# A projection of twelve matmuls dealt out in four pieces between the taps of a sampled stencil

## What is computed

```python
x = x + _L0_conv_ref(_gn(x), ...)        # deformable 3x3 convolution, 8 groups
t = t + _L1_attn_ref(_ln_t(t), L1_attn_W)  # attention over the 1024 pixels of an image
t = t + _L1_ffn_ref(_ln_t(t), ...)       # top 2 of 8 experts, per image, layer norm
```

```python
xp = x @ in_w + in_b
x1 = silu(batch_norm(depthwise_conv3x3(x)))
offset = x1 @ off_w + off_b
mask = softmax((x1 @ mask_w + mask_b).reshape(N, H, W, G, P), -1)   # G = 8, P = 9
samples = _bilinear_sample(img, sg)      # xp at 9 shifted points of each pixel and group
out = (samples * m).sum(-1)
return out @ out_w + out_b
```

## Time and profile before

| | us |
|---|---|
| median of 3 runs | 719.99 |
| lowest, highest | 719.28, 720.27 |
| the profiled execution | 716.8 |
| its span | 714.9 |
| PE, DVE, POOL, ACT busy in it | 588.3, 580.3, 304.6, 227.3 |

### The profile page before, as it was taken

One profiled execution on the slowest core, in us unless ns is written; L12 is line 12 of the kernel. 1 busy time (PEld: TensorE's weight loads), 2 busy tenths in 40 slices (PEclk: granted clock), 3 DMA queues, 4 the chain that ended last, 5 costly groups with the idle time before them and its releaser, 6 DMA issues.

```text
span 714.9 us, 11099 instructions
## 1 busy us (share of the span) xinstructions
PE 588.3 (82%) x3456; PEld 440.8 (62%) x3456; DVE 580.3 (81%) x1052; ACT 227.3 (32%) x334; POOL 304.6 (43%) x326
## 2 busy tenths in 40 slices
PE   5973877869859959969968689889999999939995
PEld 4542656558547547557547577667777777725674
DVE  4589999998999997998999999826777766652766
ACT  6150602413315205205207000234545444413431
POOL 6524794897448792058068240201222121115111
PEclk9996999998999988989999679999999999967998
DMA  6067403003003006000000000000000000004111
GB/s 184 30 260 255 141 1 104 3 1 105 1 1 105 2 2 257 1 1 2 1 1 3 0 1 1 0 1 1 1 1 1 1 1 0 1 9 110 30 45 44
DMA packets 25594, 30.54 MB, mean 43 GB/s; under 512 B 5188, under 2 KB 17684, under 8 KB 25556
## 3 DMA queue, kind: packets, MB, share of 16 engines
q1 hardware_dynamic: 24654, 29.77, 12.6%
q0 software_dynamic: 896, 0.23, 0.4%
q10 hardware_dynamic: 6, 0.00, 0.0%
HBM read 24.94 MB, written 5.05 MB: 42 GB/s over the span
## 4 chain that ended last, share of the span: by engine, by line
PE 54%; DVE 21%; issue 11%; DVEq 2%; ACT 1%; POOL 0%; POOLq 0%; ACTq 0%
PE banks L797 13%; DVE prod L1389 9%; PE banks L910 8%; PE pair L890 8%; PE pair L966 4%; PE pair L750 4%; PE banks L900 4%; PE banks L1000 3%; DVE stencil L1365 3%; DVE outer L1359 3%; PE banks L819 2%; PE pair L743 2%; PE banks L816 1%; PE banks L882 1%; PE banks L861 1%
## 5 line engine op out<-in xcount | busy, mean ns | idle before, releaser
L797 PE MATMUL banks<-ident,prod 128*128 128x128 f32 x1568 | 224.6, 294 | 82.6 <-DVE prod L1389 81.6
L797 PEld LDWEIGHTS banks<-ident,prod 128*128 128x128 f32 x1568 | 191.5, 152 | 137.8 <-DVE prod L1389 114.4
L1389 DVE TENSOR_TENSOR prod<-shifted,stencil 128x1024 f32 (+1 forms) x224 | 238.4, 1086 | 14.9 <-PE banks L797 14.6
L1157 POOL CAST far_list_i<-far_list 1x8 int32<-1x8 f32 x8 | 40.2, 5026 | 105.9 <-DVE far_list L1375 86.5
L1185 POOL TENSOR_TENSOR rstd_now<-mv_now,neg_half 128x2 f32<-128x2 f32 x32 | 23.0, 718 | 132.6 <-DVE mv_now L1441 132.6
L750 PE MATMUL pair<-xg,dw_diag 128*128 128x512 f32 x144 | 72.7, 606 | 1.2 <-ACT dw_diag L514 1.2
L910 PEld LDWEIGHTS banks<-shifted 128*128 128x128 f32 x512 | 60.2, 192 | 8.1 <-issue 6.1
L910 PE MATMUL banks<-shifted 128*128 128x128 f32 x512 | 63.2, 277 | 2.3 <-ACT shifted L651 1.4
L1359 DVE TENSOR_TENSOR outer<-hats 128x800 f32<-128x800 f32 x64 | 63.2, 987 | 0.8
L1365 DVE TENSOR_TENSOR stencil<-stencil,outer 128x800 f32 (+1 forms) x64 | 62.9, 982 | 0.3
L890 PE MATMUL pair<-shifted 128*128 128x512 f32 x128 | 60.8, 597 | 0.7 <-ACT shifted L634 0.6
(11 more groups left out here) (230 smaller groups left out, 837.0 us busy)
## 6 DMA issues: line engine op xcount, KB each, us to landing
shifted<-padded SPq DMA_DIRECT2D x42, 256.0 KB
shifted<-padded SPq DMA_DIRECT2D x14, 640.0 KB
res<-in_x_dram SPq DMA_DIRECT2D x4, 512.0 KB, 5.8
padded<-stage SPq DMA_DIRECT2D x4, 512.0 KB, 2.6
stage<-in_L_ffn_W_dram SPq DMA_DIRECT2D x16, 128.0 KB, 2.1
out_dram<-res SPq DMA_DIRECT2D x8, 256.0 KB, 2.3
padded<-stencil SPq DMA_DIRECT2D x2, 228.0 KB, 2.5
got<-padded,cell_now POOLq DMA_INDIRECT x28
```

The costliest lines, as they stand in the source:

```text
L797: mm = pe.matmul(acc_of(c, r), prod[:, d % PROD, r * G:(r + 1) * G, :].rearrange("p g c -> p (g c)"), ident[:, :], is_transpose=True, star ...
L1157: gp.tensor_copy(far_list_i[:, :], far_list[:, :]).then_inc(point, 1)
L1389: ins = ve.tensor_tensor(prod[:, dx:dx + n, :, :], shifted[:, dx:dx + n, bass.ds(((c % HALF) * ROWS + dy) * G, ROWS * G), :], stencil_of[: ...
```

## The change

The far sums of the chunk before move from ahead of tap 36 to ahead of tap 35. The projection of that chunk moves from ahead of tap 44, where its twelve matmuls stood in one row, to four places: the three matmuls of image 0 ahead of tap 39, of image 1 ahead of 41, of image 2 ahead of 43 and of image 3 ahead of 45. Every piece waits for the copy of the samples and for the residual of the chunk before it; only the last raises `conv_out`, for which ACT's `residual` waits. The two projections behind the last turn stay as they are, with their semaphore now named at the call.

```diff
-AT_FAR, AT_CONV, AT_SAMPLES, AT_PROJECT = 18, 22, 36, 44
+AT_FAR, AT_CONV, AT_SAMPLES, AT_PROJECT = 18, 22, 35, 39
...
-            def project(k, n0=0, n1=B):
+            def project(k, n0, n1, done=None):
                 last = isinstance(k, int) and k == CHUNKS - 1
                 pe.wait_ge(samp_t_done, k + 1)
                 pe.wait_ge(res1_done, CHUNKS - 1 if last else k + 1)
-                if n0 > 0:
+                if n0 > 0 and done is not None and n1 - n0 > 1:
                     pe.wait_ge(res1_first, 2 if last else 1)
...
-                mm.then_inc(conv_out if n1 == B else conv_first, 1)
+                if done is not None:
+                    mm.then_inc(done, 1)
...
-                    if i == AT_PROJECT and not first:
-                        project(k - 1)
+                    n, between = divmod(i - AT_PROJECT, 2)
+                    if 0 <= n < B and between == 0 and not first:
+                        project(k - 1, n, n + 1, conv_out if n == B - 1 else None)
                     add_up(k, i, i + 1)
...
-            project(CHUNKS - 2, 0, 1)
-            project(CHUNKS - 1, 0, 1)
+            project(CHUNKS - 2, 0, 1, conv_first)
+            project(CHUNKS - 1, 0, 1, conv_first)
...
-            project(CHUNKS - 2, 1, B)
-            project(CHUNKS - 1, 1, B)
+            project(CHUNKS - 2, 1, B, conv_out)
+            project(CHUNKS - 1, 1, B, conv_out)
```

## The result

The changed kernel takes 709.12 us (median of 4 runs, 706.93 to 709.60), the kernel before 719.63 us (median of 4 runs in this comparison, 716.62 to 720.27). The ratio is 0.986, with a 95% interval of 0.983 to 0.989: 10.5 us less. A second comparison, 5 runs against 17, gave 707.19 against 718.81 us, ratio 0.984 (0.981 to 0.987). The profiled execution took 709.08 us, its span 707.3 us.

A forecast was written before the change was run, and what follows sets the result against it. The stage was taken as bound by DVE, lengthened by PE where no `prod` slot was free. The profiled 716.8 us less 7.0 gave 709.8, plus 3.2 carried over to the median 713.0; range 708.5 to 718.0.

The forecast's parts named there:

- the lag rule: At a turn end, DVE's stall is the offset matmuls' delay behind `finish_silu`'s end without the first stall, plus 0.2 us.
- The floor of 0.6 us a turn end: DVE's stall with offset matmuls but no projection, as in turn 0; ACT's hat chain would hold DVE at `weigh_hats` anyway.
- The signs it named: DVE's slot waits 3.5 to 7.5 us, one stall of 0.5 to 1.5 per turn end, `finish_silu` spacing 50.1 to 51.
- Far sums zero: Four transposes moved from tap 36 to tap 35 hide in PE's wait as before: zero gain.
- switches zero: Going between transposes and projection matmuls on PE costs zero, upper bound 0.1 us each, 0.3 us a turn.
- copy of the samples in time: No piece waits for the samples' copy: 1.8 us of room ahead of tap 39 in turn 1; zero cost.
- The size, 7 us: Total saving at the turn ends, taken as the middle of 5.5 and 9.0 us.
- The full-clock sum: With PE at full clock throughout, turns 1 to 5 stall 3.0 instead of 11.8 us, turn 6's 0.2 go: 9.0 saved.
- the half-clock sum: With PE's half clock where it lay before, turns 1 to 5 stall 6.5 instead of 11.8 us: 5.5 saved.
- hidden work: Images 0 and 1, 1.6 us of PE work, go ahead of taps 39 and 41, where PE waits for DVE.
- The slower rival: Offset matmuls fall into PE's half clock, 2.92 us becoming 5.0; at three turns 6.3 us lost, 726.3 us; chance 0.07.
- The carry-over: The median before lay 3.2 us above the profiled execution, unexplained; added to the profiled forecast of 709.8 us.

The follow-up runs named there:

- the run with late offset matmuls: The changed kernel with four unread float32 matmuls ahead of the offset matmuls of turns 1 to 6: 713.61 us.
- a burst at 42: The kernel before with far sums ahead of tap 35 and the projection in one burst ahead of tap 42: 708.76 us.
- filler: The kernel before, its burst still ahead of tap 44, with eight unread float32 matmuls ahead of tap 42: 708.84 us, ratio 0.986.
- the three traces: Two traces of the changed kernel (709.12 and 707.19 us) and one with only the projection's pieces moved, far sums left ahead of tap 36 (707.40 us).

## Where the prediction was right, and where not

The prediction said 713.0 us, 708.5 to 718.0; measured were 709.12 and 707.19, the second below the range. What binds, and what a turn end costs at a given lag, were right; what brings the lag down was right only in part.

- **What binds, and the lag rule.** Right. Stall is lag plus 0.2 us in the traces of before (0.38 and 0.6, 2.38 and 2.57), after (0.38 and 0.58) and with four matmuls put in ahead (1.28 and 1.47). The one exception is turn 3, where a long lag is followed by a stall no longer than it: 275.83 - (273.29 + 0.68 - 2.31) = 4.17 us with 4.14 stalled before, and 1.28 with 1.27 in the run with late offset matmuls. Why is not known.
- **The floor of 0.6 us a turn end, and that more slots would not lower it.** Right: 0.57 us with pieces, with a burst at 42 and with filler, and where the slots came free sooner ACT's chain held DVE. That `row_max` would wait first was missed.
- **The signs it named.** Stalls of 4.0 and 3.5 us (3.5 to 7.5 were expected), one stall to a turn end, of 0.57 to 1.14 us, and 169.99 - 119.92 = 50.07 us from `finish_silu` to `finish_silu` (50.1 to 51): all near the lower edge or on it.
- **Far sums zero, switches zero, copy of the samples in time.** Right: 717.92 us with the far sums alone, no wait of PE for the copy.
- **The size, 7 us.** Too small; the term is the middle that I took between 5.5 and 9.0. The full-clock sum, 9.0 us, is what the stage shows (8.7). Two things were mis-sized in the half-clock sum. Turn 3 was put at 2.6 us, with the half clock lasting as long as before; it stalled 1.14, since the clock was back sooner (0.72 instead of 0.61). Turns 1 and 4 were put at 1.35 us each on the same ground. The stretch was at 0.99 and 1.00 in the first trace, with the half clock ahead of it, over image 0 (1.36 us from 157.23 to 158.59), and where a turn with pieces did meet 0.72, at an earlier place, it stalled 1.08 to 1.14. The 1.35 us for the old place was never put to the test; without any projection that place cost 1.01 and 1.05.
- **Which explanation.** The prediction counted hidden work (1.6 us of two images) as the step that brings the gain and the clock as its uncertainty. The filled run turns that around: the full clock alone brings all of it, with the burst in place. Its sentence that the pieces stand "before that idle time but hardly into it", and that the clock "may fall as before, or sometimes not", held: in ten of fifteen turns of the three traces PE still idled for 2.0 to 2.5 us ahead of tap 42, and in seven of the ten the clock fell behind it. What failed is the half-clock sum behind the 5.5 us, which let the half clock last as long as before (some 161 to 168 us in turn 1). In no turn with pieces did it reach `finish_silu`. Which of the pieces does that, or whether it is only that the work ahead lies otherwise, was not tried.
- **The Trainium skill** ("TensorE: Matmul & The Clock Gate", Part 1) was given both ways. Its first half, that activity releases the half rate, agrees with the filled run, where matmuls that nobody reads kept all five stretches at 1.00, and with the run without projections, which had more half clock; it does not account for 264 to 273 us of the kernel before, in the last section. Its second, that an idle spell brings the half rate back, is as general; that 2.4 us are such a spell was the prediction's own reading, and the turns shown in the last section speak against it.
- **The slower rival**, offset matmuls at half clock, did not come up: in both traces of the changed kernel they ran 2.9 us in every turn.
- **The carry-over** of 3.2 us from the profiled execution to the median was right for before and wrong for after, whose profiled execution was at its median. That is 3.2 of the 3.9 us by which 709.12 fell short of 713.0, and it stays open; for the profiled execution itself the forecast was 709.8 and the time 709.08. That this is so near is in part luck: the stage saved 8.7 us, not 7, and the later start took 2.2 us of it back while 1.0 us less lay behind.

## What to carry to other kernels

When a burst on PE delays others, look at the granted clock under it before moving it. Here eight matmuls that nobody reads, put ahead of it, held the clock up and took 9.2 of 12.6 us of waits away, as much as the rewrite. As an experiment such matmuls tell clock from backlog. Moving the real work earlier (the burst two taps, or its pieces) gave the same with nothing added, and the pieces lose less where the clock does fall. What keeps it up in the moved versions is not shown. A stall that is tied to a lag on another engine has a floor set by the next chain; find that chain before dealing out the next burst.

## What the runs showed of the hardware

**PE fully busy for 9 us at half clock.** I had expected the clock to come back soon after PE filled up. In turn 3 of the kernel before it did not, and the third stretch stands in the earlier trace rows:

```profile
264.00:267.00 3.00, 3.00 (x13) 2.32 (x12) 3.00 (x4) 0.00 (x0) 2.72 (x4) 0.50 0.02 5
267.00:270.00 3.00, 3.00 (x12) 2.32 (x13) 2.83 (x4) 0.00 (x0) 2.51 (x4) 0.50 0.18 26
```

PE was busy for 3.00 of 3.00 us from 264 to 273 and the granted clock stayed at 0.50, once through the projection and once through transposes. In turn 2 the same instructions had the clock back within the second image (the earlier trace rows show the fourth at 0.80 us). Busy time as the profile counts it does not tell when the clock returns.

**The same idle time, with a fall of the clock and without.** I had taken the idle time ahead of tap 42 for what brings the clock down, since the half clock followed on it in turns 1 to 5 of the kernel before (2.40 to 2.63 us idle, in all three traces). Tap 42 in turns 2 and 3 of the changed kernel, first trace, both times after the same pieces at full clock:

```profile
212.69 0.66 PE L797 MATMUL banks<-ident,prod 128*128 128x128 f32 x4 [2.24 <-DVE prod L1391]
```

```profile
263.04 1.11 PE L797 MATMUL banks<-ident,prod 128*128 128x128 f32 x4 [2.24 <-DVE prod L1391]
```

In turn 2 the tap took 0.66 us and the clock stayed at 1.00; in turn 3 it took 1.11 us at half clock. With the offset matmuls dealt out, the idle time was there in each of turns 1 to 5 and the clock never fell behind it. Turn 3 of that run, tap 42 and three stretches around the idle time:

```profile
266.53 0.66 PE L798 MATMUL banks<-ident,prod 128*128 128x128 f32 x4 [2.26 <-DVE prod L1397]
```

```profile
262.24:264.24 2.00, 2.00 (x17) 1.60 (x15) 2.00 (x3) 0.00 (x0) 2.00 (x1) 1.00 0.03 8
264.24:266.24 2.00, 0.02 (x1) 0.00 (x0) 1.97 (x3) 0.00 (x0) 1.91 (x4) 1.00 0.00 0
266.24:268.24 2.00, 1.71 (x13) 1.48 (x13) 2.00 (x3) 0.00 (x0) 1.91 (x3) 1.00 0.00 0
```

So an idle time of this length is neither enough to bring the clock down nor, in these traces, needed: in turn 1 of the kernel before the clock was also at half from about 151 to 154 us, behind idle times of no more than 1.4 us.
